# Local attention: mask product for the exponentials replaced by affine selections on GpSimd

## The chip, the cores and the metric

The kernel is one program on one core of a Trainium2 chip. The metric is the device time of one execution in microseconds. TensorE multiplies matrices (PE in the views, PEld for its weight loads), VectorE is DVE, ScalarE is ACT, GpSimd is POOL and SyncE (SP) issues the transfers. The five engines have a queue each, carry it out in order, and meet at semaphores.

## What is computed

16 independent sequences (batches) of 256 tokens by 256 features pass through five attentions with 16 heads of 16 features. In the kernel they are called self and cross (block 0), l1, l2 and l3, each followed by its projection, norms, and for cross and l3 an MLP. The change is in l2, the local attention; cut to what matters:

```python
def _window_mask(S):                       # WINDOW = 128
    i = jnp.arange(S)[:, None]; j = jnp.arange(S)[None, :]
    half = WINDOW // 2
    return (j >= i - half) & (j < i + half + 1)
q = (query @ Wq + bq) ...                  # 16 heads
k = (key @ Wk + bk) ...                    # one head, shared by the 16
v = (value @ Wv + bv) ...                  # one head
scores = jnp.matmul(q, jnp.swapaxes(k, -1, -2)) * scale
scores = jnp.where(keep[None, None], scores, NEG)
probs = jax.nn.softmax(scores, axis=-1)
attn = jnp.matmul(probs, v)
```

With 256 tokens in two tiles of 128, a query sees at most 64 keys to each side. So a tile of 128 keys meets only 192 of the 256 queries (`BAND`): queries 0 to 191 for the first tile of keys, 64 to 255 for the second. Inside that band two triangles are still outside the local range.

## The kernel before, in words

**Steps and order.** The work of each batch is a chain of named steps (`CHAIN`, lines 87 to 108) with some loads and key preparations beside it (`BESIDE`). `ORDER` (lines 128 to 168) is a string with one character per step. It says whose next step comes: `0` to `f` are the chains of the 16 batches, `A` to `P` the steps beside them, `s` the preparation of the weights. It was laid out beforehand, and no costs stand in the kernel. Every engine walks the same list (`SCHEDULE`) and issues its own part of each step, so the list fixes the order on each engine and how two or three batches are interleaved. An engine that waits at a step holds all its later steps.

**An attention.** Scores are computed twice. Steps `max0` to `max7` (two heads each) compute them with queries on the partitions and VectorE takes the row maxima (line 1026). `pieces0/1` on GpSimd cut the maxima into three bf16 pieces (lines 725 to 731), `turn0/1` turn them on TensorE, ScalarE copies them out, and a transfer puts them as three more rows under the queries in `query_stack`. Steps `exp0` to `exp7` (`scores_for_exp`, line 1187) compute the scores again with keys on the partitions. The additional rows subtract the maximum within the product, and ScalarE takes the exponential from PSUM to `probs` (line 807). Steps `weigh0` to `weigh3` (line 1216) multiply four heads of `probs` with the values. `weigh0` reads what `exp0` and `exp1` wrote, `weigh1` what `exp2` and `exp3` wrote, and so on. `out0/1` (ScalarE) copy the sums out. Four PSUM banks (`unit`) rotate among the `max` and `exp` steps and four buffers among the `exp` steps in `probs`.

**The mask.** For self, cross and l2 the mask gets into a `max` bank by ScalarE (`pre` steps, line 792). For the `exp` steps it gets there by a product with an identity matrix. In l2 that is line 1202 (the band as weights, the identity twice as moving columns, 384 columns) and `set_bits`, line 1156, which adds 128 columns. It touches the 2 x 64 columns of the bank that the band leaves out, with a product that is not the mask. Both run once per tile of keys, 16 batches x 8 steps x 2 tiles = 256 times. Then come the two score products of 192 columns (line 1211). For l2 the ScalarE instruction takes 2 x 192 = 384 columns, and the products of `weigh` read the band only (lines 1238 to 1246).

**GpSimd** computes the norms' reciprocal roots (lines 648 to 652), adds biases (line 662), spreads values (line 657), turns masks into numbers (line 666) and cuts the maxima. In the preparation it builds the identity and the band with `affine_select` (lines 621 to 629). It has no part in the `exp` and `weigh` steps.

Of the kernel before, what the change touches and what calls it, by code (L numbers as in the profile page):

```python
# [67 lines left out]
for _name in BIAS_SOURCES:  # L68
# [23 lines left out]
    "self.mix0 self.outT self.proj self.ln self.lnb self.lnT cross.q cross.qsplit cross.pre0 cross.max0 cross.pre2 "  # L92
# [27 lines left out]
def beside_steps():  # L120
# [7 lines left out]
ORDER = (  # L128
    "sA0AAsAs000AA0sAsBA02000B000B01AA000000000s1010B00001ss020A0B000s0001B00B10011B1s1101Bs100A11C1B0111"
    "0s1B1A0101s111s1C11000001101110s100sC1s000C0C010002001C120100100201s22B2122202021B10000020D222021200"  # L130
    "122220210222201C00C111021D21CC1s012102111021110D1C2101201221121A110100A10211100121111211s1001C120100"
    "12102011120002C120200011000000110B22B001020222010201212222022202220222122212212221212122121122010112"
    "01221121021100E21100200210120E0C1011Cs01021000012100201000212D02111000000000111011200121111012110111"
    "101A101111212201A11110221012212012120121202202BB2212222212020020220020102000210020001220000001110202"
    "0222022212222022202221210222000222D222222201D12212112012102010111D233112331121203333C313C2211113D321"
    "1D33D11313321312303E3323131133333313231231E32ED1E122212432D2324334433223ED2142243422434432224244E442"
    "E2443222443224434324424444F34241344E44E42434443E4324334343334333323423E2F24333F434333F42444353F44445"
    "333343442343G434343544GF45344344534334534535533F553D5D34333445444F3F45455453F5445355554F35455F454545"
    "555553453F45553355543345333453335545343553434334333E5553555E3533535543553555454F5H5F3553555453445544"
    "43545445554545354443545445444445455354433435434533543335333533343354353454533DD33445343444H445343333"  # L140
    "45444434444345E4344444E34444444544544455453545455453543345544553535455445555355535534G53443434444444"
    "5434344354334433344434543433343543G3544334333543354335533453554555345333554GG55G4GG3435HG53555H336HH"
    "575455666H55555547536666H6665H566655566G6567675656665666667F7767675H777557F66656666777777H5G77657576"
    "76777677377H7575H775755775776755575575775656555765775555555G56557777767I75767757777I7H777J7577577767"
    "I76H77577I76577I67656767566765668767686756866686766668766866666766868876688788J6878666778856677GG786"
    "866878678876876888788867688887786876777I67867II88II7878I777786I668767666766766788776667I768676878666"
    "76668767888788886788887888I68888I8867877688788777678888767878778876778786767878686788687688668668678"
    "7787777877H787866H787666766887G6G7666787666668766668676768667888678667876888668786888887886766788867"
    "87J7677677678778778787676676668776686776767667766867686676666887766678668I8I6876688678J88J78J6887686"
    "8886a869889878J9988K8888888889989889K9898Ka89898698968998J9J99J899899K8999KJ99a99J8998898K8989888987"  # L150
    "89a998899888K89KaaKL89a8a88a9aa889a88aJaa8a89aLa8Ka9aaaa98aaa8Laa9aaaK89a98a99a899aL89989899L8Lb99aa"
    "9L99aKa9a9b9ab9bK999b8b99bbbb9LbbbbLab9Maa999bab999bbLa99bbabMb9ab9b9b9ab9Lb9aa899aa99ba9bbbb9b9baJ9"
    "abaa9Jbaa9abaL9aaabaa9baaaabaLaab99baaaba9ab999aaa9ba9a9b9ba99aa9a99baLbbab99Lb9abb9abbabbNbabbb99ba"
    "9b9b9b9baab9abbabKbbKa99ababb9bMb9bbba9bba9a9bbba9babaabaa9b9a9ab99ba99baa9baababaaaaa9bab9aa99ab999"
    "ab999bJ999999J99a9999M9b9bN9b9a99bba9bba9bbbb9b9baba9bbabbbbbb9bba9aba9aaabbaaaa9aaab9aa9aaKaaKbLaab"
    "aaa9a99Laaaaaa9a9a9aba9a99ba9b99a9a9a99b9b9bb9b9b9aba9a99bbbba99b9bbabbbb9abba9bb9bbbb9bbbbb9b9bbab9"
    "a9a9aabMb9cabaaabaaMcccaNbaMbaa9cacbacacbcacbacacMcab9cacMaacacccbaacbcMcbNMacccccacccabcccbccababcb"
    "cNbcMbbcccMabcabbbcbcbbbNacbNcaccbbcaccbcbNdcccbcbbNccbccbccObbccccObdcNdccccMcdcccMcbcccOcbcbdOdcdc"
    "cddbdcdbcNccdcbddbacddbdddcOeddccdededecdOddeceeceebedcedddeddddddcceeeededceddceeedeceedePeeeNdedec"
    "eNdeecOdeeceedccceOcccPcddbceOcedcdcedcddcdcddddedcddecOdcOdcdcOceecddcOcdeddecdceddddcddecdeeddedec"  # L160
    "ddPeecdecdeedededeceNedeNcedccdeccdceeecdecccMcceMccdcceececddeecdeeeecdececccedccecdcedccecececcecc"
    "ddecdccddcedecededdccdcdeceedddccdeOdOPdddeddcddccdccecdccccecddeccccdccddcedeedeeccececeeccecedceec"
# [102 lines left out]
def build(nc, x, ctx, x_features, ctx_features, mask_cross, mask_self, params, setup_params, out):  # L265
    stack = ExitStack()
    with stack:
# [6 lines left out]
        def sem(name):  # L274
            return stack.enter_context(nc.semaphore(name))
# [340 lines left out]
        def _(pool):  # L616
# [51 lines left out]
            def run(keys):  # L668
                for key in keys:
# [4 lines left out]
                    elif step == "inputs":  # L674
# [12 lines left out]
                        if b == 0:  # L687
                            ones_in_stack(2)
# [846 lines left out]
```

## Time and profile before

| | us |
|---|---|
| median of 3 runs | 2382.35 |
| lowest and highest of them | 2373.18, 2383.21 |
| the profiled execution, its own time | 2389.43 |
| its span, first to last instruction | 2387.3 |
| TensorE (matmul) busy | 2251.6 |
| VectorE busy | 1604.9 |
| ScalarE busy | 1515.5 |
| GpSimd busy | 529.8 |

A busy time is the union of an engine's instructions. Matmuls overlap each other in the array, so a matmul's duration in a row (its way through the array counted in) is longer than what it takes from the next one; the distance between two starts tells the latter. An execution has the times around its span, 2.1 us here, in its own time.

### The profile page before, as it was taken

Reading aid. Unit: us, or ns where it says so; the run is one execution under the profiler, and the core shown is the slowest. Engines: PE = TensorE matmul, PEld = TensorE weight load, DVE = VectorE, ACT = ScalarE, POOL = GpSimd, SP = SyncE. Lnnn points to the kernel's source line nnn. Section 1 sums busy time; section 2 is a strip of 40 time slices with the busy share of each in tenths; the row PEclk is TensorE's granted clock in tenths of the full one; section 3 lists DMA queues with packets and bytes.
Section 4 is the critical chain, followed back from the end, with each engine's and each line's share of the span. In section 5 each row is a group of like instructions: output and inputs, shape, how many; then the busy total and the mean of one; then the engine's idle time right before and its main releaser. Section 6 shows DMA issues by size and latency. Waiting matters only on the chain.

```text
span 2387.3 us, 50839 instructions
## 1 busy us (share of the span) xinstructions
PE 2251.6 (94%) x18354; PEld 1688.6 (71%) x18354; DVE 1604.9 (67%) x3312; ACT 1515.5 (63%) x3171; POOL 529.8 (22%) x1120
## 2 busy tenths in 40 slices
PE   7999999999999999999999999999999999999966
PEld 4777777777777676776767677777768686776654
DVE  6667587767767658577676767667766767587422
ACT  5675657786665667748565776566676764765532
POOL 4221122222112222121112322111332212122100
PEclk8799999999999999999999999999999999999977
DMA  8322222322212123212113322112231321122100
GB/s 241 91 82 59 71 57 64 91 69 73 68 40 58 38 82 97 61 51 69 48 42 89 87 77 70 49 51 69 65 88 52 84 55 46 51 61 55 46 1 23
DMA packets 164247, 159.22 MB, mean 67 GB/s; under 512 B 17824, under 2 KB 162720, under 8 KB 162976
## 3 DMA queue, kind: packets, MB, share of 16 engines
q1 hardware_dynamic: 164000, 155.97, 24.0%
q8 instruction: 149, 2.44, 0.4%
q14 instruction: 98, 0.80, 0.1%
HBM read 35.71 MB, written 4.19 MB: 17 GB/s over the span
## 4 chain that ended last, share of the span: by engine, by line
PE 54%; issue 24%; DVE 7%; ACT 6%; POOL 3%; POOLq 3%; DMA 1%; SPq 1%; DVEq 1%; ACTq 0%
PE work L1147 13%; PE work L1138 10%; PE unit L1211 6%; PE unit L1182 6%; PE out L1235 5%; PE unit L1207 3%; DVE neg_max L1026 3%; ACT probs L807 3%; PE work L1129 2%; PE work L1351 2%; ACT unit L792 2%; PE unit L1202 1%; POOL resid L662 1%; DMA query_stack<-max_rows 1%; POOL rstd L652 1%
## 5 line engine op out<-in xcount | busy, mean ns | idle before, releaser
L1026 DVE TENSOR_REDUCE neg_max<-unit 128x2 f32<-128x512 f32 (+1 forms) x1280 | 769.0, 655 | 270.3 <-PE unit L1182 263.3
L807 ACT ACTIVATE probs<-unit 128x512 f32<-128x512 f32 (+1 forms) x1280 | 644.9, 583 | 228.8 <-PE unit L1211 225.1
L1147 PE MATMUL work<-par,hidden_t 128*128 128x256 f32 x1792 | 421.0, 385 | 7.4 <-ACT hidden_t L743 5.3
L1147 PEld LDWEIGHTS work<-par,hidden_t 128*128 128x128 f32 x1792 | 334.1, 192 | 59.1 <-ACT hidden_t L743 9.1
L1182 PE MATMUL unit<-key_stack,query_stack 96*128 96x256 bf16 x2048 | 328.2, 282 | 38.4 <-ACT unit L792 11.7
L1211 PE MATMUL unit<-query_stack,key_stack 99*128 99x256 bf16 x2048 | 351.2, 276 | 9.6 <-DMA query_stack<-max_rows 4.0
L1138 PE MATMUL work<-tok_t,par 128*128 128x256 f32 x1408 | 338.1, 387 | 5.1 <-ACT tok_t L743 3.7
L1138 PEld LDWEIGHTS work<-tok_t,par 128*128 128x128 f32 x1408 | 260.2, 193 | 43.5 <-ACT tok_t L743 8.3
L1182 PEld LDWEIGHTS unit<-key_stack,query_stack 96*128 96x128 bf16 x2048 | 178.4, 99 | 156.5 <-ACT unit L792 55.3
L1235 PE MATMUL out<-probs,values 128*17 128x256 f32 x4096 | 258.8, 384 | 4.1 <-ACT hidden_t L818 4.1
L1211 PEld LDWEIGHTS unit<-query_stack,key_stack 99*128 99x128 bf16 x2048 | 191.5, 99 | 75.3 <-ACT probs L807 16.7
L725 POOL CAST max_pieces<-neg_max 128x16 bf16<-128x16 f32 x160 | 37.4, 234 | 858.8 <-DVE neg_max L1026 858.0
L1235 PEld LDWEIGHTS out<-probs,values 128*17 128x17 f32 x4096 | 102.3, 97 | 111.0 <-issue 38.1
L792 ACT CAST unit<-neg_self 128x512 f32<-128x512 bf16 x256 | 141.2, 595 | 32.1 <-DVE neg_max L1026 31.5
L841 ACT ACTIVATE hidden_t<-work,par 128x256 f32<-128x256 f32 x256 | 107.0, 471 | 84.0 <-PE work L1138 83.4
L792 ACT CAST unit<-neg_cross 128x512 f32<-128x512 bf16 x256 | 141.5, 599 | 12.9 <-DVE neg_max L1026 12.0
L911 DVE TENSOR_TENSOR summed<-work,resid 128x512 f32<-128x512 f32 x64 | 44.1, 689 | 119.8 <-PE work L1147 119.5
L792 ACT CAST unit<-neg_band 128x384 f32<-128x384 bf16 x256 | 114.8, 493 | 13.5 <-DVE neg_max L1026 12.9
L650 POOL TENSOR_SCALAR var_eps<-mv 128x2 f32<-128x2 f32 x112 | 26.0, 232 | 416.4 <-DVE mv L882 413.1
L814 ACT CAST max_rows<-work 24x256 bf16<-24x256 f32 x160 | 57.1, 357 | 86.1 <-PE work L1319 85.6
L743 ACT COPY tok_t<-work 128x512 f32<-128x512 f32 x96 | 56.1, 586 | 84.5 <-PE work L1129 83.8
L1046 DVE TENSOR_TENSOR hidden_t<-work,recip 128x256 f32<-128x256 f32 x160 | 99.7, 623 | 12.7 <-issue 0.9
(164 smaller groups left out, 3306.8 us busy)
## 6 DMA issues: line engine op xcount, KB each, us to landing
query_stack<-query_pieces SPq DMA_DIRECT2D x480, 128.0 KB, 2.4
key_stack<-key_pieces SPq DMA_DIRECT2D x384, 128.0 KB, 2.4
c_in<-in_ctx SPq DMA_DIRECT2D x16, 256.0 KB, 3.0
tok_t<-in_x_features SPq DMA_DIRECT2D x16, 256.0 KB, 2.8
m_in<-in_mask_self SPq DMA_DIRECT2D x16, 256.0 KB, 3.1
x_in<-in_x SPq DMA_DIRECT2D x16, 256.0 KB, 3.1
ctx_t<-in_ctx_features SPq DMA_DIRECT2D x16, 256.0 KB, 3.0
m_in<-in_mask_cross SPq DMA_DIRECT2D x16, 256.0 KB, 2.8
```

What stands on the lines that cost most here:

```text
L792: a_.copy(bank[:, :, 0:n], twice(masked[:, t, 0:n], n)).then_inc(primed, 1)
L807: a_.activation(probs[:, n % PROB_BUFS, k, :, 0:width(l)], bank[:, :, 0:width(l)], ACT.Exp, scale=SCALE[l]).then_inc(exped, 1)
L814: a_.copy(max_rows[:, n % 2, :], bank[0:3 * HC, 0, :]).then_inc(taken, 1)
L841: last = a_.activation(hidden_buffer(b, l)[:, f, :], bank[:, k, :], func, bias=pv(bias)[:, f:f + 1])
L1026: v.tensor_reduce(neg_max[:, n % HALVES, t, 2 * (u % 4):2 * (u % 4) + 2], bank[:, :, 0:width(l)], AX.X, ALU.max, negate=True).then_inc(max ...
L1046: v.tensor_tensor(out_tok(b, l)[:, t, :].rearrange("p (c d h) -> p h c d", c=C, h=HC), slots[:, :, 0:HD].rearrange("p (h c) d -> p h c d", ...
L1138: last = pe.matmul(bank[:, k, :], pv(weight, C)[:, c, column + k * P:column + (k + 1) * P], src[:, c, :], start=(c == 0), stop=(c == C - 1))
L1147: last = pe.matmul(bank[:, t, :], src[:, t * P:(t + 1) * P], weight, start=(n == 0), stop=(n == len(parts) - 1))
L1182: last = pe.matmul(bank[:, i, 0:n], queries[0:ROWS, h, t * P:(t + 1) * P], keys[0:ROWS, 0 if l == "l2" else h, columns(l, t)], start=l not ...
L1207: pe.matmul(bank[:, :, t * P:(t + 1) * P], masked[:, t, k * P:(k + 1) * P], twice(ident_b[:], P), start=(t == 0), stop=False, skip_group_c ...
L1211: last = pe.matmul(bank[:, i, 0:n], keys[0:MAX_ROWS, 0 if l == "l2" else h, k * P:(k + 1) * P], queries[0:MAX_ROWS, h, columns(l, k)], sta ...
L1235: last = pe.matmul(dst, values[b % SLOTS][:, k, head_in(NJ * g + j), :], p, start=(k == 0), stop=(k == T - 1))
```

## The change

In the `exp` steps of l2 the product with the band and `set_bits` are gone, and the score products run over all 256 queries instead of the 192 of the band. ScalarE reads the band's columns of the bank and writes them to `probs` as before. GpSimd then writes zeros over the two triangles, in place, with two `affine_select` per tile of keys. They cover 2 x 64 and 2 x 128 columns, in the one or the other order. A `drain` and the increase of a new semaphore `selected` follow, and the `weigh` steps of l2 wait for that semaphore instead of `exped`. GpSimd does this at the place of the `exp` step in the common order. The selection is skipped nowhere, and other layers' steps issue what they issued. `CHAIN`, `SETUP_STEPS` and `ORDER` are new: the latter as a whole, the former two in the places shown.

```diff
 CHAIN = (
-    "self.pre7 self.max7 self.pieces1 self.exp0 self.exp1 self.exp3 self.turn1 self.exp2 ...
-    "self.out0 self.exp4 ... self.weigh3 self.out1 self.values self.mix1 "
+    "self.pre7 self.max7 self.pieces1 self.exp0 self.exp3 self.exp1 self.turn1 self.exp2 ...
+    "self.out0 self.exp4 ... self.weigh3 self.out1 self.mix1 self.values "
...
-    "l2.max5 l2.turn0 l2.max7 l2.pre6 l2.max6 l2.pieces1 l2.exp0 l2.exp2 l2.turn1 l2.exp1 l2.exp3 l2.weigh0 "
-    "l2.weigh1 l2.out0 l2.exp4 l2.exp5 l2.exp7 l2.exp6 l2.weigh2 l2.weigh3 l2.out1 l2.mix0 l2.mix1 l2.outT l2.proj "
+    "l2.max5 l2.turn0 l2.max7 l2.pre6 l2.max6 l2.pieces1 l2.exp0 l2.exp2 l2.turn1 l2.exp1 l2.exp3 l2.weigh0 l2.exp4 "
+    "l2.weigh1 l2.exp5 l2.exp7 l2.out0 l2.exp6 l2.weigh2 l2.weigh3 l2.out1 l2.mix1 l2.mix0 l2.outT l2.proj l2.gate "
...
 SETUP_STEPS = (
-    "fold par0 par1 wo_self wo_cross par2 columns_l1 par6 par7 par5 par4 turn_wo columns_l3 row_l2 row_l1 turn_bo "
-    "row_l3 bg par3 wg par8 "
+    "par0 fold wo_self wo_cross par1 par6 par3 columns_l1 par7 par2 par4 columns_l3 par5 turn_wo row_l1 row_l2 "
+    "row_l3 turn_bo bg wg par8 "
...
+SELECT_NO = Numbers(lambda l, step: step[:3] == "exp" and l == "l2")
...
+            def select_near(key):
+
+                n = EXP_NO.place[key]
+                for k in range(T):
+                    pool.wait_ge(exped, T * n + k + 1)
+                    p, edge = probs[:, n % PROB_BUFS, k], (WINDOW_HALF, P)[k]
+                    first, second = p[:, :, 0:edge], p[:, :, edge:BAND]
+                    g.affine_select(out=first, in_=first, compare_op=ALU.is_ge, fill=0.0, base=(WINDOW_HALF, 0)[k],
+                                    pattern=[[0, 2], [1, edge]], channel_multiplier=-1)
+                    g.affine_select(out=second, in_=second, compare_op=ALU.is_ge, fill=0.0, base=0,
+                                    pattern=[[0, 2], [-1, BAND - edge]], channel_multiplier=1)
+                    g.drain()
+                    pool.sem_inc(selected, 1)
...
+                    elif key in SELECT_NO.place:
+                        select_near(key)
...
-                            a_.activation(probs[:, n % PROB_BUFS, k, :, 0:width(l)], bank[:, :, 0:width(l)], ACT.Exp,
+                            a_.activation(probs[:, n % PROB_BUFS, k, :, 0:width(l)], bank[:, :, columns(l, k)], ACT.Exp,
...
-                masked = neg[l][b % SLOTS] if l in neg and l not in PRIMED_EXP else None
-                n = width(l)
+                masked = neg[l][b % SLOTS] if l in ("self", "cross") else None
...
-                    if masked is not None and l == "l2":
-                        pe.matmul(bank[:, :, 0:n], ident_b[:], twice(masked[:, k, 0:n], n), start=True, stop=False,
-                                  skip_group_check=True)
-                        set_bits(bank[:, :, n:S], S - n)
-                    elif masked is not None:
+                    if masked is not None:
...
-                        last = pe.matmul(bank[:, i, 0:n], keys[0:MAX_ROWS, 0 if l == "l2" else h, k * P:(k + 1) * P],
-                                         queries[0:MAX_ROWS, h, columns(l, k)],
-                                         start=l not in neg and i == 0, stop=i == 1, skip_group_check=True)
+                        last = pe.matmul(bank[:, i, :], keys[0:MAX_ROWS, 0 if l == "l2" else h, k * P:(k + 1) * P],
+                                         queries[0:MAX_ROWS, h, :],
+                                         start=masked is None and i == 0, stop=i == 1, skip_group_check=True)
...
-                    pe.wait_ge(exped, max(T * EXP_NO.place[b, l, f"exp{2 * g + i}"] + k + 1 for i in range(2)))
+                    done, numbers = (selected, SELECT_NO) if l == "l2" else (exped, EXP_NO)
+                    pe.wait_ge(done, max(T * numbers.place[b, l, f"exp{2 * g + i}"] + k + 1 for i in range(2)))
```

## Rows read from the trace of the kernel before

**Rows 1.** The page: span, and busy time of each engine.

```profile
span 2387.3 us, 50839 instructions
...
PE 2251.6 (94%) x18354; PEld 1688.6 (71%) x18354; DVE 1604.9 (67%) x3312; ACT 1515.5 (63%) x3171; POOL 529.8 (22%) x1120
```

**Rows 2.** The page's slices: busy tenths, and granted TensorE clock in tenths.

```profile
PE   7999999999999999999999999999999999999966
...
PEclk8799999999999999999999999999999999999977
```

**Rows 3.** The chain that ended last, shares of the span.

```profile
PE 54%; issue 24%; DVE 7%; ACT 6%; POOL 3%; POOLq 3%; DMA 1%; SPq 1%; DVEq 1%; ACTq 0%
```

**Rows 4.** Busy time in two stretches: PE, PEld, DVE, ACT, POOL, clock, DMA.

```profile
60.00:2330.00 2270.00, 2167.65 (x17872) 1636.67 (x17870) 1549.24 (x3199) 1468.36 (x3086) 496.62 (x1066) 0.98 0.23 63
728.00:736.50 8.50, 8.50 (x120) 6.84 (x119) 4.32 (x10) 6.89 (x19) 0.70 (x3) 1.00 0.56 146
```

**Rows 5.** Waits, all engines: us in total, times, longest.

```profile
ACT probs L807 <- PE unit L1211: 225.1, 159, 12.9
...
PEld unit L1182 <- ACT unit L792: 71.4, 172, 1.6
```

**Rows 6.** TensorE by line and shape: busy us, mean ns, idle before.

```profile
L1211 PE MATMUL unit<-query_stack,key_l 99*128 99x192 bf16 x512 | 84.1, 245 | 0.0
L1202 PE MATMUL unit<-neg_band,ident_b 128*128 128x384 bf16 x256 | 83.7, 327 | 0.9 <-DVE neg_max L1026 0.8
...
L1156 PE MATMUL unit<-ident_b 128*128 128x128 bf16 x256 | 55.7, 217 | 0.0
```

**Rows 7.** TensorE in order of time, two places: start, length, instruction.

```profile
284.52 0.33 PE L1202 MATMUL unit<-neg_band,ident_b 128*128 128x384 bf16 x1
284.68 0.22 PE L1156 MATMUL unit<-ident_b 128*128 128x128 bf16 x1
284.74 0.33 PE L1211 MATMUL unit<-query_stack,key_l 99*128 99x192 bf16 x2
284.91 0.33 PE L1202 MATMUL unit<-neg_band,ident_b 128*128 128x384 bf16 x1
...
1204.09 0.60 PE L1182 MATMUL unit<-key_stack,query_stack 96*128 96x256 bf16 x4
1204.52 1.03 PE L1406 MATMUL work<-norm,mean_w 128*128 128x256 f32 x4
```

**Rows 8.** GpSimd by line and shape: busy us, mean ns, idle before.

```profile
L666 POOL TENSOR_SCALAR neg_self<-m_in 128x512 bf16<-128x512 int32 x16 | 31.2, 1951 | 31.9 <-DMA m_in<-in_mask_self 29.5 <-issue 1.9 <-PE out L1235 0.2
...
L624 POOL TENSOR_SCALAR_AFFINE_SELECT summed<-summed 128x512 f32<-128x512 f32 x1 | 0.6, 629 | 0.0
...
L621 POOL TENSOR_SCALAR_AFFINE_SELECT ident<-ident 128x128 f32<-128x128 f32 x1 | 0.3, 292 | 0.3 <-issue 0.3
```

**Rows 9.** GpSimd in order of time: two instructions with a drain between.

```profile
1059.64 0.20 POOL L725 CAST max_pieces<-neg_max 128x16 bf16<-128x16 f32 x1 [3.33 <-DVE neg_max L1026]
1059.98 0.22 POOL L727 TENSOR_TENSOR max_rest<-neg_max,max_pieces 128x16 f32<-128x16 f32 x1
```

**Rows 10.** All engines in order of time: half an l2 attention.

```profile
728.97 1.65 ACT L807 ACTIVATE probs<-unit 128x384 f32<-128x384 f32 x4 [1.46 <-PE unit L1211]
...
730.75 1.60 ACT L807 ACTIVATE probs<-unit 128x384 f32<-128x384 f32 x4
...
732.06 0.52 PE L1238 MATMUL out<-probs,values_l 128*17 128x192 f32 x8
...
732.73 0.51 PE L1238 MATMUL out<-probs,values_l 128*17 128x192 f32 x8
```

**Rows 11.** Line 948: duration ns min/median/max.

```profile
L948 DVE TENSOR_TENSOR query_pieces<-query_rest,query_pieces x80: 691/693/1686, 11.4 to 2328.9; 128x512 bf16<-128x512 f32 x80
```

**Rows 12.** What GpSimd waited for: us in total, times, longest.

```profile
POOL max_pieces L725 <- DVE neg_max L1026: 858.0, 136, 24.6
POOL var_eps L650 <- DVE mv L882: 413.1, 79, 21.3
```

**Rows 13.** Who waited for line 652 on GpSimd, us, times.

```profile
  DVE norm L890: 15.5, 14
  DVE resid L906: 7.5, 29
```

More of the change, by code:

```diff
@@ L166 @@
[L166 to L167 removed]
+    "0AAAAs0s10A0AsA0BssB1001B000000A000sA000AB1s000s000A0B0B0sB1B10B110101000s0010101B10A001110Cs1A12C01"
+    "11100s11101111s10012B111s0s1sC0C00010020200100B0C00s0000B100021010200222120021202s0011200220212C0s02"
+    "22212012022020210221111C0C11C110201D21102111021C0121122011001121A110A101001C212111211C10012011s10120"
+    "120021101002C1200002101020022012100B222102B002022201220102122022022201221211122101211222112202112121"
@@ new lines @@
+    "11201201012121102100210012010020100200010210002002120012C120C000000110s21010100111211101201111110111"
+    "21201A2122120121011022A101122102202101221222222121002200210202D0102000211002B00220B00000110022010D2E"
+    "20221222220222122222021220222020212E022102120010D221120211DDD312032311321121211CC113D130312113212D11"
+    "31313123331323113332331D32331E331112213232232423223D43E433322334221E443223243324434234242232E2232444"
+    "424443244D34434244F4424D4244444242344E33244F433E33143E3EE233434E2333243E32453334F3433354244F43344333"
@@ new lines @@
+    "3543433F5444434442343454D354D434343534455F445543545354F353534555353F554F4434555553534455F5354F533544"
+    "45F5554543354334543353343355F53345335453433343335E4553H555545E345535555345F3555F3553555545445554G354"
+    "43544345554544554343443454444545435544333454435343533343335G4333353433345335345G43433454354D4444D345"
+    "334454444344345444443E3E44445454435H5454434455455444555433455554435455344555533555553453443443544454"
+    "544434344343334444433434434543334433353545333333543345333545G5553543553445543G55545GG3G5G53355753356"
@@ new lines @@
+    "6455556H65556736G666H5556556666H77665F6F66566566566676467756G67566H566HH7577357H7H67H577776657767H77"
+    "677777577757575H5677577577577557G567765755665I75776G555555655777757775777775775I67775767777775577777"
+    "7I56H7II56776H6765765675666758676776667685666678666G866666666I8766G676688786875688868867676878778668"
+    "8687868778I68786888768878877888678867877688867768778877II877767667I6I67776I666767I768667766886676666"
+    "6K6J8768888786886887888878788I8I8886788776878877768788876787787887767886777687788776867866877J677767"
@@ new lines @@
+    "876687J666766686766687766888688766766787887H6H6666667788686766878687876688868876888GG888886768768877"
+    "6788876776776777787787676677667867766766768677686676886667KJ6676688666787866I88I88676688876J8878J867"
+    "888K66J888669889878989888888J9J888979889989J8K999aaK8999K98986988999899K98998899K96K9999KJ88988898a8"
+    "88889a9JK8898889a9898aa98a898aa98a8a8L8aJaa8aa89aaK8aa9a9a8aaa8aa98aa99a9La9La899a899a89L998899989a9"
+    "a9Lab9b9aab9abK98Lb9a9babbb9b9b9b9b99a9b99Labb9ab8Mb99bbabab9bb9a999Lba9aLb9aba9aa9aaa9JaaJa99bLbbbb"
@@ new lines @@
+    "bb9b9ab9aLb9baLa9a9babaaabaaLNaaba99ba9aMaba9a9b99aab9aa99ba9b9a99aa99ba9bbab9baabbab9ba9b9b9ab9bbab"
+    "99bbKba9bbbaabbbbKbabb9a9abb9LL9bbabab9bMba9a9bbabbba9aaba9b9aa9b99ba99baa99baaabbaaaab9aJ99999999aa"
+    "bJ999baa99baba9999a99a99bbb99b99b9bbab9abb9abbb9b9b9abbbbbabaa9bbab9aNaaaaab9abbaa9aaab9aa9baaaKaaab"
+    "aKa9aa9abaa9b99aaba9aab99aM99a999abba999Lb9bbbaL999b9bb9ba9b9abbbbbb99b9b9bbb9abb99a9baabbb9bbbM99bb"
+    "abab9aMaba9aacbaabaccacababaMbaN9ccaa9acbacacabccaMabccMacaccacccbaaccbccMbcacNccacccaMbcaccbMcbabNb"
@@ new lines @@
+    "ccNcbcbbcccbabbcMabcbbcNaabcNcNbbbccbbbacbbccccdccccNbcccbbcccbbcccbcddccccbbOdccccccbcccdcdcOdccddb"
+    "ddOcbdddccbccNObcddbcedddcddeccdeedddcOecedebedddedceddcddaMeceMdeddeeedecededdceecdeeedOdNeedeeecce"
+    "eececNececdccecdccedcecOOcOcecceOedcdedcOdcdcbdcdeOdcddecdddeddcddcdeOccddddededcddddddcedePeddedecd"
+    "deceeeePdecddePedcedNcccccdcNcedcccdecccdceMPcceMedeeeecdecdeedcedeeeedeccceecdeceddccecccecceeecccc"
+    "ceddcdcdcdceddedeceddccdcecdeddceceddOOeddddddcdccdcccddcedccececcdcccdccdcedeedecccceeceeeeccdceeec"
@@ L168 @@
+    "eeedcdeedcdeeddceeddcedddeceddecdddececdedceddcedddeeedePcdeeddeedPdfefdddfddPfeeeedeededeeeefNedefN"
+    "edeeefdefedefffcffdfefefddeffefedPfPdfedfedeffffefefffPfdfdfdPffddfdfdfefffdddPdPfeffdedfedfdffedddd"
+    "dddedefOfedffdfffefeOfffffffPdfffefffffffPfdfffffeffefffdefedfeffefeedfeffdffdeeefdeffefedfdddfeeffd"
+    "efefffeeffeefffffeeeffeffffeffffffPPfffeffefefefeffdefefeffffffffffffffffeffffefefffffffffffffffffff"
+    "fffffffffffffffffffffffffffffffffffffffffffff"
 )
@@ L366, in build @@
         maxed = sem("maxed")
+        selected = sem("selected")
         primed = sem("primed")
```

39 lines of the change are left out of this document (removed), and 24 rows, old and new, of the table CHAIN.

## The prediction

> **What bounds the kernel now.** I read the page from the top. TensorE is busy 2251.6 of 2387.3 us, the others at most 67%, and GpSimd 22% [rows 1]. The slices show TensorE at nine tenths or more in 37 of 40, with the granted clock at full in nearly all of them (the higher level, 2.4 GHz); only the first two and the last two slices are thinner, and there the clock is 0.7 to 0.8 [rows 2]. The chain that ended last is 54% TensorE and 24% issue, which on a stream of matmuls is mostly TensorE as well, against 7% VectorE, 6% ScalarE and 3% GpSimd [rows 3]. So most of a microsecond taken out of TensorE's stream should come out of the time. It will not be all of it: between 60 and 2330 us TensorE is idle 2270 - 2168 = 102 us, while ScalarE waits for score products here and weight loads for ScalarE there [rows 4, 5]. TensorE is only a few banks ahead of the engines that read its scores.
>
> **What TensorE loses.** The durations in the rows by line overlap (327 ns for 384 columns [rows 6]); what counts is the distance between starts. In one tile of keys the band product starts at 284.52, `set_bits` at 284.68, the two score products at 284.74 and the next tile at 284.91 [rows 7]. A tile takes 0.39 us: 0.16 for the band, 0.06 for `set_bits`, 0.17 for two products of 192 columns. After the change two products of 256 columns are left. Four products of 256 columns of the same type take 1204.52 - 1204.09 = 0.43 us [rows 7], so two take 0.215. Saved is 0.39 - 0.215 = 0.17 us a tile, times 256 tiles [rows 6]: **43 us** (the wider score products have given back 12 of the 55 us that the two mask products take). The weight loads of the removed products lie beside the stream and bring nothing more.
>
> **What ScalarE and the PSUM banks see.** The exponential still has 384 columns, read at another offset: nothing. It begins 0.17 us sooner after its bank is free, which matters only where ScalarE waits. The exponentials outside the range have no mask below them; their values do not change a duration.
>
> **What GpSimd gets.** Two selections per tile, 128 and 256 columns. An `affine_select` of 128 columns took 0.292 us, one of 512 columns 0.629 us [rows 8], so 0.88 ns a column, and 0.40 us for 256. Together 0.69 us. Two GpSimd instructions with a drain between them have 0.14 us between the end of one and the start of the next (1059.64 + 0.20 to 1059.98) [rows 9]; I take this once a tile for drain, semaphore and wait: 0.83 us. 256 tiles are 212 us, and the engine would be busy some 710 us of 2350, so it does not bound the whole. The lower end for a tile is two rows of 0.292 us without any gap, 0.58 us. For the upper end I take the slowest row per column on this engine, 1951 ns for 512 columns [rows 8], 3.8 ns a column or 1.5 us for 384, with the gap 1.6 us. I stay with 0.83 because that is the same operation, type and two-dimensional pattern; what differs is that the rows lie 256 apart in `probs`.
>
> Of GpSimd against VectorE the trace says only that a subtraction from two SBUF tiles, 693 ns in the median, has taken up to 1686 ns [rows 11].
> The Trainium skill (SBUF — State Buffer, Who interferes with whom) says that a VectorE instruction with two SBUF inputs contends with a GpSimd instruction that reads SBUF, which is what all the new selections do. The maximum in that row agrees with it; by the rule a selection could be held for one such VectorE instruction. If one selection in eight met one and lost 0.7 us, it would be 32 x 0.7 = 22 us on GpSimd and none on TensorE.
>
> **The new wait, locally.** The average hides what happens inside an l2 attention. ScalarE makes four tiles in 1.65 us, 0.41 us a tile [rows 10]; GpSimd needs 0.83 us, twice that. In the order of before these steps stand close together: in the place shown eight tiles run from 728.97 to 732.35, `weigh0` starts at 732.06 and `weigh1` at 732.73 [rows 10]. With GpSimd behind, the eighth tile would be done at 729.4 + 8 x 0.83 = 736.0, and `weigh1` would start 3.3 us late. TensorE takes its queue in order: the score products behind it, this layer's and those of the other batches, would wait, then ScalarE and VectorE for these. TensorE was busy in all of those 8.5 us [rows 4], so it would be a loss in full. A layer has two such halves, so 16 layers x 2 x 3.3 us = 106 us if no place had more room; in many places there is more.
>
> That is what the new order has to cover. I counted in both orders what stands between `exp0` and `weigh3` of l2 and belongs to other steps: 11.0 steps in the mean before and 15.7 after. Their matmuls, by distances as above, are 6.2 us before and 10.4 after. With the layer's own products (8 steps x 2 x 0.215 = 3.4 us, three `weigh` of 0.67 us each [rows 10], and what belongs to turns) it is 16 us in the mean after, and from 10.5 to 29 us in the single layers. GpSimd needs about 0.6 us to the first exponential's end and 16 x 0.83 = 13.3 us, so 14 us until the last `weigh` may go. Six layers of the new order have 10.5 to 13.6 us there, short by 1 to 4 us each, 13 us together. Some of this the waits that are there anyway already cover, but inner places (`weigh0` and `weigh1`) can be short too. I put the new waits at **12 us** of loss. Ends: 0 us (tile of 0.58 us: 16 x 0.58 = 9.3 us fits everywhere) and, with 1.6 us a tile, 16 x 1.6 = 26 us against 16, 10 us in 16 layers = 160 us.
>
> **What queues behind on GpSimd.** At an `exp` step of l2 it now stands until ScalarE has written, and roots, biases and the cutting of maxima of other batches stand behind. They wait for VectorE for 858 and 413 us in total now [rows 12], and VectorE waits for the roots only 15.5 and 7.5 us in its two largest rows [rows 13]; so there is slack, and a step pair (1.7 us) usually goes into it. Where it does not, the cut maxima come late, then the turn, its transfer and `exp0` or `exp4` of that batch. I put 4 us on it together with the next item, bounds 0 and 20.
>
> **The new order for the rest.** The same instructions in other places. The preparation moves parameter transfers among SyncE's loads (`par6`, `par3` and `par7` forward, `par5` back), all within the first 60 us, where TensorE waits for data anyhow. The tail hardly moves: after the last batch's `weigh3` of l2 both orders have the same 36 us of TensorE work. With TensorE's stream 43 us shorter, the readers of scores have less time per bank, so part of the gain goes into the 102 us of waits. That this order is better or worse by chance I bound by 15 us to both sides, value 0.
>
> **Sum.** -43 + 12 + 4 = -27 us. The profiled execution would take 2389.4 - 27 = 2362 us; it lay 7 us above the median of the runs shown. So the median would be 2382 - 27 = 2355 us, 1.1% less.
>
> **Rivals.**
> 1. *The whole gain.* The order covers GpSimd and the layers of l2 are short nowhere: -43 us, with the order's own luck up to -55. For it: GpSimd 22% busy, more steps between `exp` and `weigh`. Against it: the six short layers and the 102 us of idle TensorE time that show coupling. Time: 2339 us.
> 2. *GpSimd bounds l2, the time rises.* One mechanism: a tile costs more than I think, each layer of l2 then lasts as long as its 16 tiles, and TensorE stands at `weigh`. The point from which it decides: the new waits must be over 43 us in 16 layers, 2.7 us a layer. A layer with 16 us of TensorE work reaches that at 18.1 us of GpSimd, (18.1) / 16 = 1.13 us a tile; for the short layers sooner, so about 1.05 us on the average. At 1.2 us a tile it is 19.2 + 0.6 - 16 = 3.8 us a layer, 61 us: 2382 - 43 + 61 = 2400 us. For it: GpSimd's rows spread up to 3.8 ns a column, and selections can be held by VectorE. Against: the same operation at 0.88 ns a column.
> 3. *TensorE's gain is hidden anyway.* ScalarE and VectorE, with two thirds of the time each, are locally full where `max` and `exp` steps stand together, and the shorter stream just waits for banks. ScalarE is busy 6.89 of 8.5 us in an l2 stretch [rows 4], and that stretch would be 8 x 0.17 = 1.4 us shorter or more; it comes near. Half the gain gone and my 16 us of waits on top: -6 us, 2376 us.
>
> **Chances.** Forecast (2345 to 2367) 0.47, rival 1 0.22, rival 3 0.18, rival 2 0.13. A change under 0.5% (12 us) can't be told from none here. Faster by more than that, below 2370.4: the forecast and rival 1 nearly whole, and a little of rival 3: 0.70. Within: most of rival 3 and the fast end of rival 2: 0.18. Slower: 0.12. Range: 2330 to 2390 us; it holds rival 1's centre with part of its luck and rival 3, and leaves out the far side of rival 2.
>
> **What would show it.** In the changed kernel's profile lines 1202 and 1156's rows for l2 are gone, the score products over `key_l` have 256 columns with starts 0.108 us apart, and TensorE's busy time falls by some 40 us or more (busy counts overlaps, so it is a bit less sure than the starts). GpSimd has 512 selections of 0.29 and 0.40 us in the mean and is busy about 710 us. The `weigh` products of l2 (line 1238's successor) have a wait row on GpSimd's selections, of about 12 us in total; ones of 43 us or more would be rival 2. The waits of TensorE for banks filled by ScalarE or VectorE grow by less than 10 us; by 20 or more it is rival 3. The prediction is wrong if a tile takes over 1 us, if `weigh` waits are far from 12 us, or if TensorE's idle time between 60 us and the tail moves by other causes more than 15 us.

## The result

| | median, us | ratio to before (95% interval) |
|---|---|---|
| before, measured beside it | 2380.26 (2373.18 to 2383.21, 4 runs) | |
| changed kernel | 2409.10 (2402.42 to 2415.36, 4 runs) | 1.0126 (1.0108 to 1.0143) |
| predicted | 2355, range 2330 to 2390 | 0.989 |

The change makes the kernel 1.3% slower, 29 us; I had forecast 27 us less. The profiled execution took 2415.36 us, its span 2413.3; it is the slowest of its four, and the profiled one of before, 2389.43 us, is slower than the four beside it as well. The ratios below leave out two executions of 3754 and 4484 us, one of e1 and one of the kernel before beside it, which stand far off all others.

The changed kernel's page has these lines in the places of [rows 1, 2, 3]: span, busy time, TensorE's slices and granted clock, and the chain that ended last.

```profile
span 2413.3 us, 50586 instructions
...
PE 2245.4 (93%) x17842; PEld 1645.7 (68%) x17842; DVE 1606.6 (67%) x3312; ACT 1520.0 (63%) x3173; POOL 718.1 (30%) x1632
...
PE   7999999999998999999999999999999999999967
...
PEclk8899999999999999999999999999999999999977
...
PE 40%; issue 21%; ACT 6%; DVE 6%; POOL 6%; POOLq 4%; DVEq 1%; DMA 1%; SPq 0%; ACTq 0%
```

TensorE has its 512 matmuls fewer, and yet the span is longer (its busy time fell by 6 us and not by the 40 that I had named as a sign): the chain has less of TensorE (54% and 24% issue before, 40% and 21% now) and more of GpSimd (3% and 3%, now 6% and 4%). The waits in the changed kernel, in total, times and longest, where [rows 5] has those of before:

```profile
ACT probs L825 <- PE unit L1224: 287.5, 191, 10.2
...
PEld unit L1200 <- ACT unit L810: 85.6, 205, 1.7
...
PEld out L1254 <- POOLq L681: 15.7, 25, 1.1
```

ScalarE waits 62 us more for scores than before, though scores for l2 take TensorE less time. That belongs to the new order, and not to TensorE's standing at `weigh`: the same wait is nearly as long in e3, which has the new order and no selections, and as short as before in e2, which has the selections in the order of before (both runs are told below):

```profile
ACT probs L823 <- PE unit L1222: 276.5, 189, 10.9
...
ACT probs L825 <- PE unit L1224: 221.9, 153, 9.8
```

`POOLq L681` is the `drain` behind the selections, ahead of the increase of the new semaphore (line 682). TensorE by line and shape, and GpSimd's selections, against [rows 6, 8]:

```profile
L1224 PE MATMUL unit<-query_stack,key_l 99*128 99x256 bf16 x512 | 76.8, 278 | 2.3 <-DMA query_stack<-max_rows 1.3 <-DVE neg_max L1044 0.7
...
L1252 PE MATMUL out<-probs,values_l 128*17 128x192 f32 x512 | 33.9, 337 | 12.8 <-POOLq L681 11.6 <-ACT hidden_t L836 0.8
L1254 PE MATMUL out<-probs,values_l 128*17 128x128 f32 x512 | 26.9, 283 | 6.3 <-POOLq L681 6.1
```

```profile
L679 POOL TENSOR_SCALAR_AFFINE_SELECT probs<-probs 128x256 f32<-128x256 f32 x128 | 60.1, 470 | 0.0
...
L677 POOL TENSOR_SCALAR_AFFINE_SELECT probs<-probs 128x128 f32<-128x128 f32 x128 | 42.3, 331 | 49.5 <-ACT probs L825 37.5 <-issue 10.6
```

And one half of an l2 attention in order of time, the place that answers to [rows 10]:

```profile
734.54 1.64 ACT L825 ACTIVATE probs<-unit 128x384 f32<-128x384 f32 x4 [1.24 <-PE unit L1224]
...
736.29 1.62 ACT L825 ACTIVATE probs<-unit 128x384 f32<-128x384 f32 x4
...
739.17 0.29 POOL L677 TENSOR_SCALAR_AFFINE_SELECT probs<-probs 128x128 f32<-128x128 f32 x1 [0.16 <-issue]
739.42 0.41 POOL L679 TENSOR_SCALAR_AFFINE_SELECT probs<-probs 128x256 f32<-128x256 f32 x1
739.99 0.41 POOL L677 TENSOR_SCALAR_AFFINE_SELECT probs<-probs 128x256 f32<-128x256 f32 x1 [0.16 <-issue]
740.02 0.52 PE L1252 MATMUL out<-probs,values_l 128*17 128x192 f32 x8 [0.92 <-POOLq L681]
...
742.40 0.29 POOL L679 TENSOR_SCALAR_AFFINE_SELECT probs<-probs 128x128 f32<-128x128 f32 x1
742.79 0.41 PE L1254 MATMUL out<-probs,values_l 128*17 128x128 f32 x8 [0.53 <-POOLq L681]
```

GpSimd takes a new tile every 739.99 - 739.17 = 0.82 us, the eighth is done at 742.69, and ScalarE had written it at 737.91. So the selections are 4.8 us behind, in a layer where the new order has put steps in between (TensorE waits only 0.92 and 0.53 us in these rows). Over the whole trace a new tile follows after 0.82 us in the median and 0.90 us in the mean, where GpSimd does not wait for ScalarE.

### The profile page after: what moved, and what is told of

Its sections match the earlier page's. It is cut to its first block, busy times and chain, and to the rows that moved or that the text cites. A ratio compares the mean times of both kernels' runs of the same rounds, so it can differ in the third digit from the quotient of the medians.

```text
span 2413.3 us, 50586 instructions
## 1 busy us (share of the span) xinstructions
PE 2245.4 (93%) x17842; PEld 1645.7 (68%) x17842; DVE 1606.6 (67%) x3312; ACT 1520.0 (63%) x3173; POOL 718.1 (30%) x1632
## 4 chain that ended last, share of the span: by engine, by line
PE 40%; issue 21%; ACT 6%; DVE 6%; POOL 6%; POOLq 4%; DVEq 1%; DMA 1%; SPq 0%; ACTq 0%
PE work L1165 10%; PE work L1156 8%; PE out L1249 5%; PE unit L1224 5%; PE unit L1200 4%; DVE neg_max L1044 3%; ACT probs L825 3%; PE work L1147 2%; PE unit L1220 2%; POOLq L681 2%; POOL probs L677 2%; ACT unit L810 2%; PE work L1365 1%; POOL rstd L654 1%; POOL resid L664 1%
## 5 line engine op out<-in xcount | busy, mean ns | idle before, releaser
L1249 PE MATMUL out<-probs,values 128*17 128x256 f32 x4096 | 263.8, 388 | 2.6 <-ACT hidden_t L836 2.6
L677 POOL TENSOR_SCALAR_AFFINE_SELECT probs<-probs 128x128 f32<-128x128 f32 (+1 forms) x256 | 96.5, 377 | 71.0 <-ACT probs L825 41.7
L1220 PE MATMUL unit<-ident_b,neg_self 128*128 128x256 bf16 x512 | 100.8, 279 | 3.9 <-DVE neg_max L1044 2.9
```

The costliest lines, as they stand in the source:

```text
L677: g.affine_select(out=first, in_=first, compare_op=ALU.is_ge, fill=0.0, base=(WINDOW_HALF, 0)[k], pattern=[[0, 2], [1, edge]], channel_mul ...
L1220: pe.matmul(bank[:, :, t * P:(t + 1) * P], masked[:, t, k * P:(k + 1) * P], twice(ident_b[:], P), start=(t == 0), stop=False, skip_group_c ...
L1249: last = pe.matmul(dst, values[b % SLOTS][:, k, head_in(NJ * g + j), :], p, start=(k == 0), stop=(k == T - 1))
```

## The experiments

Two things were changed at once, code and order, and the code has two halves. The first four runs fill the table of both orders with three codes: mask product (as before), neither, selections. Comparisons are by the ratio to the kernel before, which took 2376 to 2380 us beside them; a ratio of 0.01 is 24 us. By the intervals, the difference of two runs is known to 4 to 7 us.

**e1**: the code of before, with `CHAIN`, `SETUP_STEPS` and `ORDER` of after.

> The code of before (band product and set_bits on TensorE, no selections) with the changed kernel's order. It tells what the order alone does. The changed kernel came out at 2409 us against 2380, and TensorE's stream is some 40 us shorter, so some 66 us of idle TensorE time are new. Theory A, the selections' latency made them: the order alone costs little, 2380 to 2395 us. Theory B, the order itself is the worse one: if it made all of the 66 us, 2380 + 66 = 2446 us; half of it 2413. Theory C, TensorE's saving is hidden by ScalarE and VectorE anyway and the order costs the rest: 2380 + 29 = 2409 us.

**e2**: the code of after, with the three of before.

> The changed code (no mask product, selections on GpSimd) with the order of before. Theory A: the order of before has no room for the selections between exp and weigh; of the 106 us worked out for it perhaps two thirds are paid: 2380 - 43 + 70 = 2407 us, up to 2440, and lines of weigh show waits of 50 us or more for GpSimd. Theory B: the old order is the good one and the selections fit: 2380 - 43 + 15 = 2352 us. Theory C: 2380 to 2400 us.

**e3** (new order) and **e4** (order of before), the code of after with

```diff
-                    elif key in SELECT_NO.place:
-                        select_near(key)
...
-                    done, numbers = (selected, SELECT_NO) if l == "l2" else (exped, EXP_NO)
+                    done, numbers = exped, EXP_NO
```

> The changed kernel without the two selections, weigh waits for the exponentials directly; the local mask is left out of the probabilities, so this part of the computation is missing. Theory A: all 66 us of new idle time go away, 2409 - 66 = 2343 us. Theory B: nothing changes, 2400 to 2409 us. Theory C: the saving of TensorE does not show even so, 2385 to 2400 us.

> As the kernel before, but with neither the mask product in l2's exponential steps nor the selections (the local mask is left out of the probabilities). It measures what TensorE's 43 us are worth by themselves in the order of before. Theories A and B: nearly all, 2380 - 43 = 2337 us. Theory C: the readers of the scores bound these stretches, so at most a third, 2366 us or more.

Measured, as ratios, and in us of difference from before:

| | mask product | neither | selections |
|---|---|---|---|
| order of before | 1 | 0.9973 (0.9961 to 0.9985), -6 (e4) | 1.0576 (1.0559 to 1.0594), +137 (e2) |
| new order | 1.0140 (1.0115 to 1.0165), +33 (e1) | 1.0020 (1.0008 to 1.0032), +5 (e3) | 1.0126 (1.0108 to 1.0143), +30 (the change) |

The theories A, B and C of the expectations each had one part. C: taking the mask product out is worth 6 us of 43 in the order of before, and 33 - 5 = 28 us in the new one. B: the new order costs 33 us with the product and 11 without. A: the selections cost 137 + 6 = 143 us in the order of before and 25 in the new one. On the way to the changed kernel: -6 + 11 + 25 = +30 us.

**Why 43 us are worth 6.** Kernel e4 in order of time, at the place of [rows 10], weight loads, TensorE and ScalarE:

```profile
729.50 0.11 PEld L1222 LDWEIGHTS unit<-query_stack,key_l 99*128 99x128 bf16 x2 [0.27 <-ACT probs L823]
729.88 0.11 PEld L1222 LDWEIGHTS unit<-query_stack,key_l 99*128 99x128 bf16 x2 [0.27 <-ACT probs L823]
730.26 0.11 PEld L1222 LDWEIGHTS unit<-query_stack,key_l 99*128 99x128 bf16 x2 [0.27 <-ACT probs L823]
```

```profile
728.96 3.17 ACT L823 ACTIVATE probs<-unit 128x384 f32<-128x384 f32 x8 [0.48 <-PE unit L1222]
```

```profile
728.00:736.50 8.50, 7.21 (x88) 4.46 (x88) 6.72 (x15) 4.24 (x10) 0.00 (x0) 1.00 0.35 93
```

In this place the tiles follow each other every 0.38 us, as they did with the mask product (0.39 us [rows 7]), and ahead of each the weight load waits 0.27 us until ScalarE, at 3.17 / 8 = 0.40 us a tile, has emptied a bank. In the same 8.5 us TensorE was busy throughout before [rows 4], and is for 7.21 us now. Here the mask product had filled the time in which TensorE would have waited.

Over all 256 tiles that is the smaller part of the answer. I set the starts of TensorE's matmuls in the traces of e6 and of e4 side by side. e6 is told below: it has the mask product and a shorter exponential, took as long as before, and is nearer to the medians than the trace of before. The score tiles of l2 take 105.7 us in e6 (105.2 in the kernel before) and 78.7 in e4: 27 of the 43 us do come out there. In 151 tiles of e4 a tile takes 0.22 us, so the saving is whole; in 72 it takes 0.30 to 0.42 us as in the rows above, which is 72 x (0.38 - 0.22) = 12 us of the 16 that do not come out. The other 21 us are lost again behind the scores: 4.7 us at l2's `weigh` products, 3.9 and 3.5 at the products for the maxima of l2 and of other layers, 2.2 at the turns, 6 in smaller pieces. The clock is in these: TensorE spent 2 x (1 - 0.974) x 2369 = 123 us at its lower level in e4 and 109 in e6, so up to 7 of the 21 us. In the new order (e1 and e3) the tiles shrink from 108.9 to 69.2 us, 40 of the 43, and 28 show in the time.

e5 to e8 and e17 vary both sides of the pace, in the order of before.

**e5** (on e4) and **e6** (on before): `bank[:, :, 0:P]` instead of `width(l)` for l2's exponential.

> The order of before, neither mask product nor selections (that one took 2372 us), and the exponential of l2 covers 2 x 128 instead of 2 x 192 columns, so a part of the probabilities is left out. ScalarE's four tiles in 1.65 us are 0.40 us a tile with 384 columns; 512 columns take 0.52 us, so 256 take about 0.29. Theory C1: TensorE's tile of 0.39 us was matched with ScalarE's tile of 0.40 us, so the saving on TensorE could not show; once ScalarE needs 0.29 us a tile, some 0.11 x 256 = 28 us come out: 2345 us. Theory C2, the saving is lost in other places (pieces, transfers, VectorE): 2365 to 2372 us.

> The kernel before with the mask product, and only the exponential of l2 cut to 2 x 128 columns (a part of the probabilities is left out). Theory C1: TensorE's 0.39 us a tile is now the longer one, so ScalarE's relief brings little alone, 2370 to 2379 us, though both reliefs together bring 30 us or more. If ScalarE alone bounded these stretches in the kernel before (theory C3), it would be 2379 - 28 = 2351 us.

**e7** (on before): `dense(...)[0:FC - 3 if l == "cross" else FC]` in `hid_out`.

> The kernel before, with 3 of the 8 chunks of cross's second MLP product left out (this part of the computation is missing): 16 x 2 x 3 products of 0.43 us are 41 us less of TensorE, as much as the mask products, but in a step where no PSUM bank of scores turns. Theory C1, the loss is local to l2's exponential steps: nearly all of it shows, 2379 - 35 = 2344 us. The rival, that TensorE is not the bound anywhere and its savings are worth a sixth in general: 2372 us.

**e8** (on before) and **e17** (on e4): `PRIMED_MAX = ('self', 'cross')`, the score products for l2's maxima over all keys with `start=True`, the maximum over `bank[:, :, columns(l, t)]`, and nothing done at l2's `pre` steps.

> The order of before and the mask product for the exponentials, but l2's maxima are taken over the unmasked band: ScalarE no longer copies the band to the banks (256 copies of 384 columns, 0.45 us each with the gaps, about 102 us less of ScalarE), and TensorE's score products for the maxima have 256 instead of 192 columns (13 us more). The maximum over more keys still cancels in the division. Theory C1: ScalarE is the partner that sets l2's pace, so this is faster, 2379 + 13 - 30 = 2362 us. If TensorE alone bounds: 2379 + 13 = 2392 us.

> The order of before with neither mask product nor selections (local mask left out of the probabilities, 2372 us) and no priming of l2's banks by ScalarE, maxima over the unmasked band. With the mask product, no priming gave 2381 us: 13 us more of TensorE and 5 us more of time, so 8 us of relief. Theory C1, ScalarE holds TensorE's saving back: relief and saving together bring much more than 7 + 8 us beyond the 13: 2379 + 13 - 43 = 2349 us or less. If the priming has no part in it: 2372 + 5 = 2377 us.

| | ratio | us |
|---|---|---|
| e6, shorter exponential, mask product | 1.0006 (0.9994 to 1.0017) | +1 |
| e5, shorter exponential, neither | 0.9927 (0.9911 to 0.9943) | -17 |
| e7, 41 us less in the MLP | 0.9842 (0.9827 to 0.9857) | -38 |
| e8, no priming, mask product | 1.0020 (1.0009 to 1.0030) | +5 |
| e17, no priming, neither | 0.9968 (0.9956 to 0.9980) | -8 |

e7 refutes that TensorE's time counts little in general: 38 of 41 us come out where no bank of scores turns. Relief of ScalarE alone is worth nothing (e6), relief of TensorE alone 6 us (e4), both together 17 (e5). That is C1's mark, two engines in step. Its size is not: I expected 2345 us and got 2360, and of the 11 us between e4 and e5 only 4 lie at the score tiles (78.7 and 74.5 us). In e8 and e17 TensorE has, by my estimate, 13 us more to do, and both come out 8 us and more below 2379 + 13 and 2379 - 6 + 13. But e17 stays at -8 us, so the priming is not what holds the rest. What is left is spread over many short waits, as above; the trace of e5 still has weight loads of l2's scores waiting for ScalarE, for VectorE and for the transfer of the maxima in similar amounts:

```profile
L1222 PEld LDWEIGHTS unit<-query_stack,key_l 99*128 99x128 bf16 x512 | 43.5, 99 | 30.5 <-ACT probs L823 8.4 <-DVE neg_max L1042 6.6 <-DMA query_stack<-max_rows 6.6
```

**What in the selections costs.** e9 (new order) and e10 (order of before) keep GpSimd's wait and time at each tile, but free `weigh` from it:

```diff
-                    g.affine_select(out=first, ...)
-                    g.affine_select(out=second, ...)
+                    g.tensor_tensor(spare[:], spare[:], minus_half[:], ALU.pow)
...
-                    done, numbers = (selected, SELECT_NO) if l == "l2" else (exped, EXP_NO)
+                    done, numbers = exped, EXP_NO
```

> The changed kernel, but at each tile GpSimd, after its wait for the exponential, computes one root of 2 columns in a tile of its own (0.72 us, about as long as the two selections) instead of the selections, and weigh waits for the exponential alone (the local mask is left out). It separates GpSimd's being occupied and standing in its queue from TensorE's wait for it. Without either it took 2384 us, with both 2409 us. Theory W, the wait at weigh is the cost: 2384 to 2387 us. Theory Q, the roots and cut maxima behind it on GpSimd come late: 2400 us or more.

> The same in the order of before, where the selections cost 143 us on top of 2372 us. Theory W: 2372 to 2380 us. Theory Q: at least a third of the 143 us, 2420 us or more.

A tile of this stand-in follows the last one after 0.87 us in the median and 0.91 us in the mean, so it is no lighter than the selections (0.82 and 0.90).

**e11** (order of before) and **e12** (new order): both selections on `p[:, :, 0:16]` and `p[:, :, 64:80]`.

> Selections in the order of before, each cut to 2 x 16 columns (the local mask is mostly left out): by 0.18 us + 0.88 ns a column two of them take 0.42 us, 0.56 us with the gaps, instead of 0.82 us a tile. Theory R, the loss is the amount by which GpSimd is slower than ScalarE's 0.40 us a tile, summed over the tiles in a row: (0.56 - 0.40) / (0.82 - 0.40) = 38% of 143 us, 2372 + 55 = 2427 us. Theory L, the loss is the fixed way from ScalarE by GpSimd to TensorE: nearly all of it remains, 2490 us.

> The same in the changed kernel's order (2384 us without selections, 2409 us with them). Theory R: 38% of 25 us, 2394 us. Theory L: 2405 us. If the new order's distances cover the shorter selections wholly: 2384 us.

| | ratio | us above "neither" of that order |
|---|---|---|
| e9, busy only, new order | 1.0062 (1.0045 to 1.0080) | 10 of 25 |
| e10, busy only, order of before | 1.0202 (1.0187 to 1.0217) | 54 of 143 |
| e11, short selections, order of before | 1.0244 (1.0229 to 1.0258) | 64 of 143 |
| e12, short selections, new order | 1.0027 (1.0016 to 1.0038) | 2 of 25 |

With no wait at `weigh` at all, GpSimd's being occupied costs some 40% of what the selections cost. The views of waits of e4 and then e10 show where (us in total, times, longest):

```profile
DVE norm L906 <- POOL rstd L654: 15.6, 14, 1.5
...
PE work L1331 <- POOL max_pieces L747: 12.2, 18, 1.5
```

```profile
DVE norm L905 <- POOL rstd L656: 43.7, 16, 8.7
...
PEld work L1330 <- POOL max_pieces L746: 40.6, 35, 5.1
...
PE work L1330 <- POOL max_pieces L746: 30.4, 24, 4.7
```

GpSimd waits in its queue for ScalarE's exponential, and the roots and cut maxima of other batches stand behind it: single waits of 1.5 us have become 8.7 and 4.7 us.

These 40% are not a part of the loss with the selections in place, though. The same views of e2:

```profile
PE out L1252 <- POOLq L681: 89.2, 41, 7.1
...
PE work L1333 <- POOL max_pieces L749: 15.3, 19, 2.9
```

Where TensorE stands at `weigh` anyway, it hardly waits for what queues behind on GpSimd: 15.3 us for the cut maxima, against 30.4 in e10 and 12.2 in e4. The starts of the matmuls, set side by side as above, say the same. Of the 142 us between the traces of e4 and e2, 125 arise at l2's `weigh` products. Of the 31 us between e3 and the changed kernel, 25.5 arise there and 3.5 at the two products that follow the norms' roots. So the wait at `weigh` makes nearly all of the loss in both orders. The queue would cost 10 and 54 us alone; the two costs overlap and do not add.

e11 has 45% of the loss where theory R said 38% and theory L, a fixed way, nearly all: it goes by how much slower than ScalarE a tile is on GpSimd, and hardly by the fixed way; where the distances cover the shorter tile (e12) it is gone within the error.

**Room in the order.** For e13 (selections), e14 (neither) and e15 (mask product) I delayed 47 of l2's 64 `weigh` steps in the order of before, with the steps of l2 that must stay behind them, its next `exp` steps among them.

> The selections with the order of before, in which only l2's weigh steps (47 of 64) and what must stay behind them are put some steps later, until 1.5 us of TensorE's work stand between the exponentials' score products and the weigh. Everything else keeps its relative order. Theory W2, room before weigh is what the new order has ahead: much of the 143 us goes, 2515 - 60 = 2455 us or less. Rival, it is the place of the exp steps among GpSimd's other steps that counts, not the weigh steps: 2500 us or more.

> That order with neither mask product nor selections (the local mask is left out), which took 2372 us in the order of before. If spreading l2 among the other batches is what costs in the new order (12 us there, 2384 us), a part shows here: 2378 us. If it costs nothing, or lets TensorE's saving show, as the 28 us between mask product and none in the new order suggest: 2355 to 2370 us.

> That order with the code of before, mask product included. Spreading costs by itself: 2390 us or more (the new order has 2412). It doesn't: 2375 to 2382 us, and the 33 us of the new order come from its other changes.

Measured 1.0604 (1.0587 to 1.0620), 1.0308 (1.0288 to 1.0328) and 1.0269 (1.0254 to 1.0283): +144, +73 and +64 us. e13 looks like a refutation of W2, by which room before `weigh` is what helps; but with nothing of the selections in it this order is already 73 us slower, so the selections cost 71 us in it instead of 143. TensorE's matmuls wait 34.6 + 4.9 = 39.5 us at `weigh`, and 89.2 + 6.4 = 95.6 in e2. Room halves their price, and this crude way of making it costs as much. e14's expectation missed the latter; e15's had it as one of two outcomes (2390 us or more). Part of e14's 73 us is the clock again (0.957, see the last section). The new order makes its room far more cheaply, for 11 us without the product. Why it costs 11 and not nothing was not tested: against e6, e1's trace has its 35 us more spread over many kinds of products, none with over 10.

**e16**: in the changed kernel GpSimd does the selections at the `weigh` step.

```diff
-                    elif key in SELECT_NO.place:
-                        select_near(key)
+                    elif l == "l2" and step[:5] == "weigh":   # both exp steps of this weigh, in order
...
```

> The changed kernel with the same selections, but GpSimd does those of two exp steps at the place of their weigh step in the common order instead of at the exp steps, so that roots and cut maxima in between go first. Theory Q (12 of the 25 us are GpSimd's queue): they come back, 2397 us. Rival: the later start of the selections makes TensorE wait longer than the queue gave, 2415 us or more.

1.0628 (1.0607 to 1.0650), +149 us, 119 above the changed kernel. TensorE's waits for the selections are most of it (of the 108 us between the two traces, 99 arise at l2's `weigh` products):

```profile
PE out L1256 <- POOLq L681: 94.7, 36, 6.4
```

While a finished tile lies there for selection, GpSimd stands for 112 us waiting for other engines, VectorE above all, at the roots, maxima and biases that now go first; in the changed kernel that is 6 us. So the selections come far too late. Theory Q had also started from 12 us of queue in the changed kernel, of which the trace shows some 3. The rival was right, in kind and not in size.

**e18**: the changed kernel without the priming, as e8 is the kernel before without it.

> The changed kernel (selections, new order) without the priming of l2's banks: the reference is still computed. ScalarE loses 102 us, TensorE gains 13 us. In the new order TensorE's stream counts more (28 of 43 us showed) and the selections lag by GpSimd, which this does not touch: 2409 + 10 - 10 = 2409 us. If ScalarE's lag is what the weigh steps of l2 wait for as well: 2385 us or less, near the kernel before.

1.0148 (1.0133 to 1.0163), +35 us; nothing gained. No version that does the whole computation beat the kernel before: e4, e5, e7 and e17, the faster ones, leave part of it out.

## Why the prediction was wrong, step by step

- *"Most of a microsecond taken out of TensorE's stream should come out of the time"*, -43 us: this step failed. The tile was read rightly: 0.17 us saved (0.22 us a tile in 151 tiles of e4), 512 matmuls gone. It is worth 6 us in the order of before and 28 in the new one, while 41 us in the MLP are worth 38 (e7). Of the 37 us that are missing in the order of before, 12 are ScalarE's pace. I had that row in hand, ScalarE's 0.41 us a tile beside TensorE's 0.39, and used it for GpSimd's lag and not for TensorE's gain. The larger part is lost in short waits behind the scores and, up to 7 us, at the lower clock; the prediction had put nothing on these. I had the outcome as rival 3, too small (half the gain gone) and with 0.18. Its sign, 20 us more of waits for banks, is met by the weight loads (140 us on the `unit` rows before, 167 now) and not by the matmuls (25 and 28).
- *The selections' duration*, 0.83 us a tile: measured 0.82 in the median, 0.90 in the mean. GpSimd busy 718 us, forecast about 710. In the estimate beside it one selection in eight is 64 of 512 and not 32, so 45 us by its own terms; in the trace a pair takes 0.73 us in the mean and 0.65 in the median, 20 us in 256 pairs, from whatever cause.
- *The new waits at `weigh`*, 12 us, and *what queues behind on GpSimd*, 4 us with coupling: together 25 us, nearly all of them at `weigh`. The matmuls' rows there have 11.6 + 6.1 = 18 us. The bounds 0 and 160 held. That a layer short by 1 to 4 us is the only place to pay was too kind. For the order of before I had worked out 106 us; it is 143, with up to half of it by way of the clock.
- *The new order for the rest*, 0 +- 15 us: +11 without the product, inside the bound, and +33 with it, outside.
- *Sum*: -43 + 16 + 0 = -27 forecast; -6 + 25 + 11 = +30 measured. Of the 57 us between, 37 are the first step, 11 the order, 9 the waits. Taken the other way round, the order first and then the product, it is -28 + 25 + 33, and they are 15, 33 and 9: 22 us belong to code and order together, and the runs can't divide them.
- *Rival 2*, the only one on the right side, was said to need 1.05 us a tile. The time rose at 0.82 to 0.90, because there was no gain of 43 us to use up first; the break-even point was worked out with the same wrong term.

## What to carry to other kernels

Before a product is taken off the busiest engine, compare its time per tile with that of the engine that empties the same banks: where they are in step, the saving does not come out. Then ask where the engine waits next; a share of 94% busy did not keep 43 us from being worth 6. A step put on an idle engine with an in-order queue is paid by whoever waits for it, and where nobody does, by whoever stands behind its wait; slower per tile than its supplier, it needs an order with room, and the same code can cost 25 or 143 us by the order. Code and order changed together are to be measured in a table of both.

## What the runs showed of the hardware

Waits on TensorE cost again through its clock. In e2 the mean granted clock is 0.948, in e4, which differs by the selections, 0.974. Since it has two levels, that is 2 x (1 - 0.948) x 2511 = 261 us at the lower one, 1.2 GHz, against 123 us. Four stretches of e2 in columns as [rows 4], and two rows of TensorE in order of time:

```profile
1205.00:1211.80 6.80, 5.87 (x38) 4.10 (x37) 6.13 (x11) 3.29 (x9) 2.04 (x5) 1.00 0.54 143
1211.80:1218.20 6.40, 0.39 (x6) 0.14 (x9) 3.00 (x9) 0.59 (x2) 4.45 (x13) 0.68 0.01 3
1218.20:1224.00 5.80, 5.80 (x61) 3.30 (x61) 1.26 (x2) 1.74 (x4) 3.14 (x10) 0.50 0.00 0
1224.00:1230.00 6.00, 3.51 (x40) 2.17 (x39) 3.14 (x9) 2.16 (x6) 4.89 (x13) 0.97 0.01 3
...
1221.23 1.04 PE L1224 MATMUL unit<-query_stack,key_l 99*128 99x256 bf16 x4
1222.06 1.06 PE L1200 MATMUL unit<-key_stack,query_stack 96*128 96x256 bf16 x4
```

TensorE stands at `weigh` for 6.0 of the 6.4 us of the second, and runs at half clock through the third, although it is busy in all of it. Four score products of 256 columns take 1222.06 - 1221.23 = 0.83 us in that stretch and 0.43 at the higher level [rows 7], so work takes twice as long, and the 138 us more at it can account for up to half of that, 69 of e2's 143 us. By the same working it is up to 31 us in e10 (0.962), up to 44 of e14's in the same comparison (0.957), and in the changed kernel (0.970, against 0.974 in e3) up to 10 of the 31 us between the two traces.

Two selections of one tile overlap on GpSimd: the second starts 0.25 us after the first, which lasts 0.29 us, and so the rows' means, 331 and 470 ns, are together more than the 739.83 - 739.17 = 0.66 us that the pair takes. In lines 677 and 679 one selection takes from 285 to 945 ns; what the long ones met was not tested.
